# A quantiser's comparison chain recast as seven independent compares on VectorE and a tree of adds on GpSimd

## The reference

```
x = x + attn(layernorm(x))        # 16 heads of 64, RoPE, causal softmax, Wo
x = x + ffn(layernorm(x))
ffn: gate = fp4_linear(x, w_gate); y = fp4_linear(x, w_up)
     out  = fp4_linear(silu(gate) * y, w_down)         # 1024 -> 2816 -> 1024
fp4_linear(x, w) = q(x) @ q(w).T
q(x): blocks of 16 along the last axis
      scale = max(max|x| / 6, 1e-12)
      idx   = searchsorted([.25 .75 1.25 1.75 2.5 3.5 5], |x / scale|)
      q     = [0 .5 1 1.5 2 3 4 6][idx] * sign(x) * scale
```

## Time and profile before

| | |
|---|---|
| time, median of 3 runs | 4291.27 us (4290.65 to 4293.37) |
| the profiled execution | 4288.06 us |
| its span on the slowest core (core 2) | 4286.5 us |
| spans of the 8 cores | 4275.7 to 4286.5 us |
| mean granted TensorE clock of the cores | 0.616 to 0.619 |
| DVE busy | 2630.4 us, 61% of the span |
| PE busy | 1909.3 us, 45% |
| ACT busy | 1138.1 us, 27% |
| POOL busy | 54.1 us, 1%, all of it four memsets and the issue of DMAs |

### The profile page before, as it was taken

The page is one execution under the profiler, slowest core; times in us unless marked ns, Lnnn a source line. Parts: engine busy times, 40 slices in busy tenths (PEclk is TensorE's granted clock), DMA queues, the critical chain, the costliest instruction groups (busy, mean ns, idle before and its releaser), DMA issues.

```text
span 4286.5 us, 30447 instructions; the slowest of 8 cores (4275.7 to 4286.5 us)
## 1 busy us (share of the span) xinstructions
PE 1909.3 (45%) x6809; PEld 704.5 (16%) x6864; DVE 2630.4 (61%) x4886; ACT 1138.1 (27%) x1936; POOL 54.1 (1%) x104
## 2 busy tenths in 40 slices
PE   1544543445444444454356544444444444444444
PEld 0211111112111111111111231111111111111111
DVE  2275574764756747557463307777777777777776
ACT  4332331333323323233133342111111111111111
POOL 0000000000000000000000000000000000000000
PEclk9855556556565565555656656666666666666666
DMA  2001001110110100100102430000000000000000
GB/s 84 30 30 44 22 30 37 30 44 15 30 37 25 35 30 27 42 21 28 35 27 100 155 106 10 15 10 10 10 11 10 10 10 10 10 10 10 10 10 5
DMA packets 49103, 131.56 MB, mean 31 GB/s; under 512 B 8610, under 2 KB 16930, under 8 KB 48803
## 3 DMA queue, kind: packets, MB, share of 16 engines
q1 hardware_dynamic: 39012, 95.51, 7.9%
q0 software_dynamic: 9920, 34.09, 2.0%
HBM read 95.50 MB, written 34.08 MB: 30 GB/s over the span
## 4 chain that ended last, share of the span: by engine, by line
DVE 51%; PE 23%; ACT 9%; issue 9%; DMA 7%; DVEq 1%; ACTq 0%; SPq 0%; POOLq 0%
PE psO L625 3%; PE psA L486 2%; PE psB L486 2%; DVE qbmF L153 2%; DVE quE L177 2%; DVE qcA L220 2%; DVE qcB L195 2%; DVE qcA L204 2%; DVE qcB L213 2%; DVE quF L177 2%; DVE qcAF L220 2%; PE psC L592 2%; DVE qcBF L213 2%; DVE qcBF L195 2%; DVE qcAF L204 2%
## 5 line engine op out<-in xcount | busy, mean ns | idle before, releaser
L625 PE MATMUL psO<-PT,vaug 128*65 128x512 bf16 x576 | 360.0, 625 | 321.1 <-DVE PT L618 255.9
L1022 PE MATMUL psO<-wdqT,hqT_t 128*128 128x512 bf16 x688 | 295.6, 604 | 83.1 <-ACT hqT_t L1011 69.8
L609 ACT ACTIVATE PT<-psC,nb 128x512 bf16<-128x512 f32 x320 | 219.5, 686 | 378.5 <-PE psC L592 378.2
L618 DVE TENSOR_TENSOR PT<-PT,mskb 128x512 bf16<-128x512 bf16 x192 | 79.1, 422 | 360.7 <-ACT PT L609 360.0
L1003 PE MATMUL psT<-idn_b,hqb 128*128 128x128 bf16 x352 | 45.0, 263 | 419.3 <-DVE qbmF L153 375.9
L177 DVE TENSOR_TENSOR quE<-qxs,qr 128x1024 f32<-128x1024 f32 (+1 forms) x68 | 81.2, 1194 | 228.4 <-ACT qxs L156 226.0
L982 PE MATMUL psT<-idn_b,xqb 128*128 128x128 bf16 x128 | 16.2, 306 | 455.8 <-DVE xqb L243 455.8
L486 PE MATMUL psA<-wqkvp,xlT 128*128 128x384 bf16 x512 | 105.0, 353 | 211.6 <-DVE wqkvp L475 211.6
L592 PE MATMUL psC<-QTr,KTr 64*128 64x512 bf16 x320 | 193.0, 603 | 10.7 <-ACT KTr L574 10.7
L609 ACT ACTIVATE PT<-psD,nb 128x512 bf16<-128x512 f32 x256 | 175.6, 686 | 80.0 <-PE psD L592 79.5
L592 PE MATMUL psD<-QTr,KTr 64*128 64x512 bf16 x320 | 194.7, 609 | 0.0
(11 more groups left out here) (176 smaller groups left out, 4367.1 us busy)
## 6 DMA issues: line engine op xcount, KB each, us to landing
wstg<-wqkv SPq DMA_DIRECT2D x8, 1536.0 KB, 9.4
wfE<-wg SPq DMA_DIRECT2D x22, 512.0 KB, 4.1
wfE<-wu SPq DMA_DIRECT2D x22, 512.0 KB, 4.0
x_a<-x SPq DMA_DIRECT2D x16, 512.0 KB, 3.4
wfE<-wd SPq DMA_DIRECT2D x16, 512.0 KB, 4.0
x_c<-x SPq DMA_DIRECT2D x16, 512.0 KB, 3.9
xscr<-x1b POOLq DMA_DIRECT2D x16, 512.0 KB, 3.4
x_t<-xscr SPq DMA_DIRECT2D x16, 512.0 KB, 4.0
```

Of the source, the lines that this page charges most:

```text
L609: c.activation(PT[:, kcp % 4, :], ps[:], AFT.Exp, bias=nb12.ap(), scale=0.125)),
L625: return te.matmul(av_banks[abk], vaug.ap()[:, kcp, hh, :], PT[:, kcp % 4, :], start=(kcp == 0), stop=(kcp == nkc - 1), skip_group_check=True)
L1022: ins = te.matmul(psO[:, nh * 512:(nh + 1) * 512], hqT_t.ap()[:, j, :], wdqT.ap()[:, j, nh * 512:(nh + 1) * 512], start=(j == 0), stop=(j ...
```

## The change

In `quant_chain` the seven compares become seven independent `tensor_scalar` instructions, each with u alone as input, which write a 0/1 mask (for the last three thresholds multiplied by 2, 2 and 4 in the same instruction). Six additions in three levels then sum the masks, on POOL: three, then two, then one, with a wait on a new semaphore sPOOL between the levels. The multiplication by the block scale on DVE waits for the last of them. Two more buffers per set (qp6, qp7) hold masks. In the feed-forward stage the separate output tiles outb go: the residual add writes into x_t, the store reads x_t, and the load of x_t two tiles later waits for that store.

```diff
-        def c3a(v):
+        def c3A(v):
             u = qu.ap()[:, 0:F]
             v.tensor_scalar(qa[:, 0:F], u, TH[0], None, Alu.is_gt)
-            v.tensor_scalar(qc_[:, 0:F], u, TH[4], None, Alu.is_gt)
+            v.tensor_scalar(qb_[:, 0:F], u, TH[1], None, Alu.is_gt)
+            v.tensor_scalar(qc_[:, 0:F], u, TH[2], None, Alu.is_gt)
+            v.tensor_scalar(qt_[:, 0:F], u, TH[3], None, Alu.is_gt)
+            v.tensor_scalar(xsq[:, 0:F], u, TH[4], 2.0, Alu.is_gt, Alu.mult)
+            v.tensor_scalar(p6[:, 0:F], u, TH[5], 2.0, Alu.is_gt, Alu.mult)
+            v.tensor_scalar(p7[:, 0:F], u, TH[6], 4.0, Alu.is_gt, Alu.mult)
             return v.tensor_scalar(s2[:, 0:F], sg[:, 0:F], 2.0, -1.0,
                                    Alu.mult, Alu.add)
-        va = sch.add("vector", c3a, waits=[(sDVE, v2)] + list(waits3),
+        va = sch.add("vector", c3A, waits=[(sDVE, v2)] + list(waits3),
                      inc=sDVE)
-        def c3b(v):
-            u = qu.ap()[:, 0:F]
-            v.scalar_tensor_tensor(qb_[:, 0:F], u, TH[1], qa.ap()[:, 0:F],
-                                   Alu.is_gt, Alu.add)
-            return v.scalar_tensor_tensor(qt_[:, 0:F], u, TH[5],
-                                          qc_.ap()[:, 0:F],
-                                          Alu.is_gt, Alu.add)
-        vb = sch.add("vector", c3b, waits=[(sDVE, va)], inc=sDVE)
...
-        ve = sch.add("vector", (lambda v: v.scalar_tensor_tensor(
-            qa[:, 0:F], qt_.ap()[:, 0:F], 2.0, qb_.ap()[:, 0:F],
-            Alu.mult, Alu.add)), waits=[(sDVE, vd)], inc=sDVE)
+        def pl1(g):
+            g.tensor_tensor(qa[:, 0:F], qa.ap()[:, 0:F], qb_.ap()[:, 0:F],
+                            Alu.add)
+            g.tensor_tensor(qc_[:, 0:F], qc_.ap()[:, 0:F], qt_.ap()[:, 0:F],
+                            Alu.add)
+            return g.tensor_tensor(xsq[:, 0:F], xsq.ap()[:, 0:F],
+                                   p6.ap()[:, 0:F], Alu.add)
+        p1v = sch.add("gpsimd", pl1, waits=[(sDVE, va)], inc=sPOOL)
+
+        def pl2(g):
+            g.tensor_tensor(qa[:, 0:F], qa.ap()[:, 0:F], qc_.ap()[:, 0:F],
+                            Alu.add)
+            return g.tensor_tensor(xsq[:, 0:F], xsq.ap()[:, 0:F],
+                                   p7.ap()[:, 0:F], Alu.add)
+        p2v = sch.add("gpsimd", pl2, waits=[(sPOOL, p1v)], inc=sPOOL)
+        p3v = sch.add("gpsimd", (lambda g: g.tensor_tensor(
+            qa[:, 0:F], qa.ap()[:, 0:F], xsq.ap()[:, 0:F], Alu.add)),
+            waits=[(sPOOL, p2v)], inc=sPOOL)
...
-        vf = sch.add("vector", c3f, waits=[(sDVE, ve)], inc=sDVE)
+        vf = sch.add("vector", c3f, waits=[(sPOOL, p3v)], inc=sDVE)
...
             if t >= 2:
                 wx.append((sDVE, prev_epi))
+                wx.append((sFO[r], out_dma[t - 2]))
...
             prev_epi = sch.add("vector", (lambda v, r=r: v.tensor_tensor(
-                outb[r][:], x_t[r][:], psO[:], Alu.add)), waits=epw, inc=sDVE)
-            out_dma[t] = dma("gpsimd", sFO[r], out_v[:, t, :], outb[r][:],
+                x_t[r][:], x_t[r][:], psO[:], Alu.add)), waits=epw, inc=sDVE)
+            out_dma[t] = dma("gpsimd", sFO[r], out_v[:, t, :], x_t[r][:],
                              waits=[(sDVE, prev_epi)])
```

More of the change, by code:

```diff
@@ L112, in build_nc @@
     sDVE = Sem(root.enter_context(nc.semaphore("sDVE")))
+    sPOOL = Sem(root.enter_context(nc.semaphore("sPOOL")))
     psA = root.enter_context(nc.psum_tensor("psA", [128, 512], F32))
@@ L146, in quant_chain @@
     def quant_chain(bufs, F, src, soff, dst, doff, waits1, waits3):
-        (qu, qt_, qa, qb_, qc_, sg, s2, bm, sh, rb, bmc, rb2, xsq) = bufs
+        (qu, qt_, qa, qb_, qc_, sg, s2, bm, sh, rb, bmc, rb2, xsq, p6, p7) = bufs
         nb = F // 16
@@ L387, in build_nc @@
         qxs = mksb(stEq, "qxs", [128, FQ], F32, side=R)
+        qp6 = mksb(stEq, "qp6", [128, FQ], F32, side=R)
+        qp7 = mksb(stEq, "qp7", [128, FQ], F32, side=R)
         bufsE = (quE, qtE, qcA, qcB, qcC, qsg, qs2, qbm, qsh, qrb, qbc,
-                 qr2, qxs)
+                 qr2, qxs, qp6, qp7)
         wjobs = []
@@ L926, in build_nc @@
         hqT_t = mksb(stF, "hqT_t", [128, NJ, 128], BF16, side=R)
-        outb = [mksb(stF, f"outb{i}", [128, D], F32, side=R) for i in range(2)]
         FQ2 = 512
@@ L944, in build_nc @@
                 mksb(stF, f"qxsF{i}", [128, FQ2], F32, side=R),
+                mksb(stF, f"qp6F{i}", [128, FQ2], F32, side=R),
+                mksb(stF, f"qp7F{i}", [128, FQ2], F32, side=R),
             ))
```

## The result

The changed kernel takes 5403.62 us (median of 8 runs, 5400.61 to 5405.6) where the kernel before takes 4290.41 us (8 runs, 4288.13 to 4293.37): a ratio of 1.2595, 95% interval 1.2581 to 1.2608, slower. The forecast was 5440 us, the range 5150 to 5720. The profiled execution took 5400.29 us (span 5398.7).

What follows compares the result with a forecast made beforehand. The prediction took DVE, idle in order behind POOL's six adds, to bound the kernel. Attention +573 and feed-forward +580 us made +1153 on the profiled 4288: 5441, forecast 5440 us, range 5150 to 5720.

Steps and rivals of the forecast that it cites:

- The bound: DVE in both stages: nearly every microsecond added to a chain, or taken from it, moves the end.
- Rival 3: Half of the attention's growth is hidden behind ACT and PE working on the next query block; 5153 us, chance 0.05.
- slack of 7 us: Attention: three times DVE waited for ACT after a chain, by at most 2.4 us; 3 x 2.4 subtracted.
- The masks: DVE's seven compares: masks ready 4.79 us after the first compare at 1024 columns, 2.77 at 512; multiplying costs nothing.
- POOL's add: Each of six adds takes twice DVE's two-input pass: 2.28 us at 1024 columns, 1.22 at 512.
- Rivals 1, 2 and 4: On POOL's add: 1 as fast as DVE, 4545 us, 0.08; 2 below break-even, 4147, 0.03; 4 at three times, 6336, 0.07.
- The waits: Hand-overs DVE to POOL, POOL on itself twice, POOL to DVE: 0.15 + 2 x 0.17 + 0.25 = 0.75 us a chain.
- The edits at nothing: The x_t store and load edits cost nothing; a possibly lower TensorE clock, 10 us, was left to the range.
- theory A: For the reorders: DVE and POOL work side by side without hindering each other; about 4730 us for e8, 4300 for e9.

Runs made afterwards that it cites:

- e2: The changed kernel with one of POOL's six adds left out (the mask of the last threshold is not summed); 5106.87 us, ratio 1.1895.
- e7: The changed kernel with masks and sums in bf16, the adds still on POOL; 5235.91 us, a single run.
- e4: The changed kernel with the six adds moved to DVE and masks and sums in bf16; 4129.19 us, ratio 0.9619.
- e3: The kernel before with only the x_t edits (outb gone, store from x_t, load waits for that store); 4291.4 us, ratio 0.9999.
- e9: As e8, with the attention's chains also reordered so DVE works on beside POOL's adds; 4622.96 us, ratio 1.0785.
- e8: The changed kernel, feed-forward only: next chain's front issued ahead of the waiting multiplication, transposes and down projection one piece later; 5054.64 us, ratio 1.178.

## Why the prediction was right, step by step

- **The bound.** DVE's chains set the end, as read from the earlier trace rows, and nothing overtakes the instruction that waits: e2 came out 300 us shorter than the change for 300 us of adds taken away. Rival 3 (half hidden in the attention) falls with it; the attention grew by 560 us where 573 were predicted, slack of 7 us taken off.
- **The masks.** Predicted ready 4.79 us after the first compare starts; POOL starts 4.80 us after it. The compares that also multiply (L191 to L193) have the pitch of the others, 0.60 us, so costing the multiplication at nothing was right. ("3 to 5 us a chain", what the change would win without the adds, is 3.3 to 5.7 by the prediction's own numbers, 6.06 - 2.77 and 10.46 - 4.79; nothing else hangs on it.)
- **POOL's add.** Predicted 2.28 and 1.22 us; the pitch is 2.30 (2688.47 - 2686.17) and 1.22 us. The factor of 2 on DVE's two-input row, which no row proved, is 2.0 at both widths. That it came out so well is in part luck: the rows of before allowed anything from a compare to a division, and the reason given for 2, operands fetched one after the other, is tested by no run. In bf16 the factor is some 3.5 at 1024 columns (2.106 us a pass on POOL in e7 against a pitch of 0.61 on DVE in e4), so 2 is the factor for f32. Rivals 1, 2 and 4 (factors 1, under 0.7 and 3) fall by that pitch alone. The Trainium skill's 1.96 for this operation (GPSIMD Engine Reference, "Performance versus the Vector engine") agrees with the traces: 2.329 us a pass on POOL against 1.225 on DVE is 1.90.
- **The waits.** This term was too large. With the add at its measured pitch, 19.09 - 4.79 - 6 x 2.30 = 0.50 us is left at 1024 columns and 10.62 - 2.77 - 6 x 1.22 = 0.53 at 512, not 0.75. The prediction took 0.15 us for the way from DVE to POOL and 0.25 for the way back, the latter from PE's start after DVE. But POOL starts 4.80 us after the first compare, only 0.01 after the 4.79 forecast for the masks; and from POOL to DVE it is 2700.46 - 2700.36 = 0.10. POOL's wait on its own result was right at 0.17. Over 196 chains some 0.23 us make 45 us, and the add's 0.02 us a pass above the forecast at 1024 columns takes some 8 of them back. That leaves 37 of the 40 us between 1153 predicted and 1113 measured.
- **The edits at nothing.** e3 shows the x_t part at nothing. TensorE's granted clock fell from 0.67 to 0.63 in the feed-forward stage; the chains alone (112 x 4.56 + 16 x 2.53 = 551 us, the latter from a 256-column chain of 6.38 us against 3.85) already give the 553 by which the stage grew, so the lower clock cost next to nothing here.
- **What it did not see.** The rivals asked how fast POOL is, not whether POOL and DVE can work side by side. In this kernel they never try, since DVE waits, so the forecast did not need it. Whoever had hidden the wait on the strength of the same numbers alone (theory A, about 4300 us for e9) would have found 4623 us, 334 above the kernel before.

## What to carry to other kernels

Moving work from a busy engine to an idle one saves nothing if the busy one, issuing in order, then waits for the result: price the added wait as the full time of the moved work on the other engine, plus the hand-overs, here 0.50 to 0.53 us. Before hiding such a wait by a reorder, look whether the two engines slow each other; here more than half of the hidden time came back as longer DVE passes. What made the recast pay was neither: the masks and their sums are small whole numbers that fit a narrower type, and on DVE that nearly halved the price of the adds (4129 us against 4290 before). Whether the old running sums would have gained in bf16 as well was not tried. They also read u, which stays f32, and the rows speak against it: a pass that reads one f32 and one bf16 operand, as the last multiplication of a chain does, takes 0.68 us at 512 columns (L237), as much as hmat with f32 operands alone (L1073), and not 0.42 like the masks in bf16.

## What the runs showed of the hardware that I had not expected

- POOL's add and some of DVE's passes exclude each other. Passes of two inputs and one-input f32 tensor_scalar passes wait for the end of an add (0.42 becomes 1.23 and more), while the reduction (0.69) and the reciprocal (0.35) go on undisturbed. POOL's adds are longer there too, 1.26 to 1.65 us. All this is read from the rows of e8 and e9. The Trainium skill, in SBUF — State Buffer, section "Who interferes with whom", says that the two engines share one pair of ports, that it is held for a whole instruction, and that a VectorE instruction with two SBUF inputs, or in a two-port mode, contends while a reduction doesn't. The traces of e8 and e9 agree: masks of 1308 ns instead of 423.
- POOL's add goes mainly by the element: 2.33, 1.26 and 0.72 us at 1024, 512 and 256 columns in f32, and still 2.11 and 1.15 us at 1024 and 512 in bf16. The steps between the f32 widths are 2.1 ns an element, with 0.18 to 0.19 us beside them.
- By the rows of the changed kernel, the hand-over from POOL to DVE is short, 0.10 us; from DVE to POOL it is 0.16 us (2686.17 after L194's end at 2686.01), and POOL's wait on its own result costs 0.17 us (L209 starts 2.47 us after L204, an add's pitch being 2.30).
